# A graph network's second message layer in three sum passes, with the degree sums taken from TensorE

## The chip, the core and the metric

The kernel runs as one program on one core of a Trainium2 chip. The metric is the device time in microseconds (us) of one execution; lower is better. Engines are called by the profile's names: PE is TensorE (PEld its weight loads), DVE VectorE, ACT ScalarE, POOL GpSimd, SP the queue that issues most DMAs.

## What is computed

3125 nodes of 128 features, 100,000 edges (`src`, `dst`). First a block of two message layers, then a graph U-Net of nine convolutions ("in", three "dn", "bot", three "up", "out"). The change sits at the end of the first block and the beginning of the "in" convolution:

```
def _priv_conv(h, src, dst, n, Wl, bl, Wr, scale):
    xn = _l2norm(h)
    agg = jax.ops.segment_sum(xn[src], dst, num_segments=n)
    h_norm = jnp.linalg.norm(h, axis=-1, keepdims=True)
    out = _l2norm(agg) * h_norm * scale
    out = out @ Wl + bl + h @ Wr
    return _l2norm(out)
...
x = x + _L0_gnn_ref(h, ...)            # two such layers, 128 -> 256 -> 128 features
h = jnp.maximum(_layernorm(x, axis=-1), 0.0)
...
deg = 1.0 + jax.ops.segment_sum(ew, dst, num_segments=n)      # gcn_conv
dinv = jax.lax.rsqrt(deg)
norm = dinv[src] * dinv[dst] * ew
```

## The kernel before

The nodes are padded to 25 tiles of 128 (`TILES`). The program first builds the dense adjacency matrix in SBUF as 8-bit floats (`adj`: on the partitions the source within its tile, along the row tile after tile 3200 destinations, 3136 = `COLS` of them in use, self loops included; an entry is the count of edges times 0.125). Every `segment_sum` is then a product on PE: for each source tile t two f16 parts of the rows (high and low, `parts1[:, t, k]`) times `adj`'s row of t, in blocks of 448 destinations, 7 blocks (`BLOCKS`), each block a PSUM bank that gathers over the 25 tiles. PE keeps at most 7 such banks.

Layer 1 (`first_layer`) projects tile by tile: PE L2390, then DVE L1250, L1251 and the squares L1069, whose two tensor inputs are the same tile of SBUF. Layer 2 has 256 features in, m = 0 and 1. `fast_aggregate` (L2260) sums m = 0 in two passes of 4 and 3 blocks, then m = 1 likewise; DVE copies each finished block out of PSUM (L1049, `blocks_of`), and a pass waits until the banks that it writes were copied. PE is strictly in order, and so are the other engines: each is a queue written out by hand, with semaphores (`wait_ge`) between them.

After the last pass comes `second_layer`: PE projects the tiles two by two (L2344: sums times Wl, own rows times Wr), with the norms of the sums (L2271) after the fourth pair; DVE adds the bias (L1159) and combines (L1170, `combine`), ACT takes squares (L1971, `unit_squares`), DVE adds x (L1183, `add_x`), ACT squares again (L1978, `center_squares`), DVE makes the layer norm's factors (`scale_rows`), ACT writes the rows (L1986, `second_rows`), PE transposes them (L2363) and ACT keeps them (L1999). This goes in two parts of tiles, `LN_PARTS`. Between, PE sums the degrees (`degree_sums(0, False)`, L2305): 25 x 25 products of a 128x128 piece of `adj` with a column of ones. DVE turns them to 1/sqrt (L1031 to L1033).

Then `unet` begins with "in": PE products with the weight (L2762, groups of four tiles), ACT and DVE scale and split them to f16 (L2000, L1710), PE sums in three passes of 4, 2 and 1 blocks (L2800). DVE takes the blocks with `d_all`, the 1/sqrt degrees on every partition, which go out to DRAM (`dk_dram`) and come back broadcast. SP loads x again into `nodebuf` for `add_x`; in the kernel before this is done early, when `nodebuf` is free after the input's layer norm.

## Time and profile before

| | us |
|---|---|
| median of 3 runs | 1125.64 (1122.07 to 1128.34) |
| the profiled execution | 1124.67 |
| its span in the trace | 1122.5 |
| PE busy | 936.8 (83%) |
| DVE busy | 572.8 (51%) |
| ACT busy | 396.0 (35%) |
| POOL busy | 79.9 (7%) |

Times in the rows count from the start of the span. The profiled execution's own time is 2.2 us more than its span. The mean granted clock of PE is 0.918 of its full 2.4 GHz; the level under it is 1.2 GHz, 0.50 in the rows. A matmul's duration in a row is longer than its share of the engine, since matmuls are pipelined; a run of them is read by its length and count.

### The profile page before, as it was taken

Reading aid. Unit: us, or ns where it says so; the run is one execution under the profiler, and the core shown is the slowest. Engines: PE = TensorE matmul, PEld = TensorE weight load, DVE = VectorE, ACT = ScalarE, POOL = GpSimd, SP = SyncE. Lnnn points to the kernel's source line nnn. Section 1 sums busy time; section 2 is a strip of 40 time slices with the busy share of each in tenths; the row PEclk is TensorE's granted clock in tenths of the full one; section 3 lists DMA queues with packets and bytes.
Section 4 is the critical chain, followed back from the end, with each engine's and each line's share of the span. In section 5 each row is a group of like instructions: output and inputs, shape, how many; then the busy total and the mean of one; then the engine's idle time right before and its main releaser. Section 6 shows DMA issues by size and latency. Waiting matters only on the chain.

```text
span 1122.5 us, 17876 instructions
## 1 busy us (share of the span) xinstructions
PE 936.8 (83%) x7347; PEld 608.7 (54%) x7347; DVE 572.8 (51%) x1630; ACT 396.0 (35%) x869; POOL 79.9 (7%) x102
## 2 busy tenths in 40 slices
PE   0346999998799999979999978988876785778997
PEld 0335666766555556965465545655535443454654
DVE  4799999986921011642120267545542654445222
ACT  1538999982661000372010031544104402220300
POOL 2100000000000000000000000741014100020000
PEclk9759999999899999859999999998988787889999
DMA  6430000007100000011000002774114200140002
GB/s 192 136 84 1 1 2 1 2 1 318 49 1 1 1 1 1 2 68 52 1 1 1 1 1 61 258 214 141 27 25 119 60 1 1 30 175 29 33 1 59
DMA packets 39794, 60.39 MB, mean 54 GB/s; under 512 B 3822, under 2 KB 30721, under 8 KB 39192
## 3 DMA queue, kind: packets, MB, share of 16 engines
q1 hardware_dynamic: 31202, 38.17, 10.3%
q0 software_dynamic: 4592, 17.86, 5.2%
q10 hardware_dynamic: 3910, 3.12, 1.1%
q8 instruction: 61, 1.00, 0.4%
q14 instruction: 29, 0.24, 0.1%
HBM read 33.08 MB, written 30.85 MB: 57 GB/s over the span
## 4 chain that ended last, share of the span: by engine, by line
PE 55%; DVE 32%; ACT 5%; DMA 4%; issue 3%; POOL 1%; ACTq 0%; DVEq 0%; POOLq 0%; SPq 0%
PE psum L2800 24%; PE psum L2260 12%; DVE region L1010 7%; DVE region L1003 6%; PE psum L2568 4%; PE psum L2165 2%; DVE region L1517 2%; PE psum L2762 2%; DMA half_table<-region 2%; PE psum L2344 1%; PE psum L2190 1%; DMA nodebuf<-in_x 1%; POOL region L778 1%; DVE region L1251 1%; PE psum L2782 1%
## 5 line engine op out<-in xcount | busy, mean ns | idle before, releaser
L2800 PE MATMUL psum<-adj,region 128*128 128x448 fp8e4 x1050 | 201.8, 353 | 0.0
L2800 PEld LDWEIGHTS psum<-adj,region 128*128 128x128 f16 x1050 | 102.5, 98 | 92.9
L2260 PE MATMUL psum<-adj,region 128*128 128x448 fp8e4 x700 | 135.5, 355 | 3.1 <-DVE region L1244 3.1
L2190 PE MATMUL psum<-region 128*128 128x200 bf16 (+2 forms) x1176 | 111.0, 229 | 20.6 <-DVE region L1010 20.5
L2190 PEld LDWEIGHTS psum<-region 128*128 128x128 bf16 x1176 | 93.2, 99 | 55.0 <-DVE region L1010 30.4
L2260 PEld LDWEIGHTS psum<-adj,region 128*128 128x128 f16 x700 | 68.7, 98 | 66.8 <-issue 5.2
L2800 PE MATMUL psum<-region 128*128 128x448 fp8e4 (+2 forms) x426 | 83.7, 359 | 13.6 <-DVE region L1710 13.5
L1862 ACT ACTIVATE adj<-psum 128x400 fp8e4<-128x400 f32 x196 | 86.7, 518 | 19.4 <-PE psum L2194 18.8
L1010 DVE TENSOR_TENSOR region<-iota_key,region 128x1200 bf16<-128x1200 bf16 x147 | 92.7, 703 | 0.0
L2165 PE MATMUL psum<-adj,region 128*128 128x448 fp8e4 x350 | 91.7, 355 | 0.0
L778 POOL DMA_INDIRECT region<-adj_table,node_of x33 | 31.2, 945 | 848.3 <-DVE node_of L1647 731.3
L1003 DVE TENSOR_TENSOR region<-iota_lo,region 128x3072 bf16<-128x3072 bf16 x49 | 87.0, 1775 | 0.3 <-PE psum L2194 0.2
L2000 ACT ACTIVATE region<-psum 128x512 fp8e4<-128x512 f32 (+6 forms) x111 | 61.8, 599 | 71.5 <-PE psum L2782 24.9
L1736 DVE SCALAR_TENSOR_TENSOR region<-psum,unfit,region 128x448 f32<-128x448 f32 (+2 forms) x31 | 19.4, 661 | 123.4 <-PE psum L2800 107.5
L2568 PE MATMUL psum<-adj,nodebuf 128*128 128x448 fp8e4 x350 | 77.5, 376 | 0.4 <-issue 0.4
L1517 DVE CAST region<-psum 128x512 fp8e4<-128x512 f32 (+2 forms) x87 | 47.1, 599 | 58.8 <-PE psum L2645 29.4
L1845 ACT ACTIVATE region<-adj,below_full 128x3200 fp8e4<-128x3200 fp8e4 (+1 forms) x25 | 72.7, 2906 | 0.1
L2800 PEld LDWEIGHTS psum<-region 128*128 128x128 f16 x426 | 43.1, 102 | 51.4 <-issue 17.2
L2194 PE MATMUL psum<-ident 128*128 128x8 bf16 x392 | 67.5, 172 | 0.0
L2000 ACT ACTIVATE region<-psum,dcol 128x128 f16<-128x128 f32 x82 | 23.1, 377 | 121.2 <-PE psum L2762 104.3
L2078 ACT ACTIVATE region<-region,bn 128x512 f32<-128x512 f32 (+7 forms) x16 | 14.2, 948 | 126.1 <-DVE bn L1778 126.1
L1710 DVE SCALAR_TENSOR_TENSOR region<-psum,dcol,region 128x128 f16<-128x128 f32 x82 | 22.8, 345 | 67.5 <-ACT region L2000 67.5
(348 smaller groups left out, 1209.0 us busy)
## 6 DMA issues: line engine op xcount, KB each, us to landing
adj_table<-adj SPq DMA_DIRECT2D x1, 10000.0 KB, 27.2
edge_table<-edges SPq DMA_DIRECT2D x1, 4656.0 KB
region<-dk_dram SPq DMA_DIRECT2D x2, 1568.0 KB, 8.3
adj_table<-region SPq DMA_DIRECT2D x1, 2704.0 KB, 8.9
half_table<-region SPq DMA_DIRECT2D x2, 832.0 KB, 7.1
node_table<-region SPq DMA_DIRECT2D x1, 1650.0 KB, 8.4
xs_dram<-nodebuf SPq DMA_DIRECT2D x1, 1600.0 KB, 6.1
nodebuf<-xs_dram SPq DMA_DIRECT2D x1, 1600.0 KB, 6.1
```

Of the source, the lines that this page charges most:

```text
L1003: nc.vector.tensor_tensor(hot_lo[:, r].rearrange("p c j n i -> p (c j) n i"), iota_lo[:].rearrange("p (o n) i -> p o n i", o=1).broadcast_ ...
L1010: nc.vector.tensor_tensor(hot_key[:, r, c, :, k0:k1, :], iota_key[:, k0:k1, :].rearrange("p (o n) i -> p o n i", o=1).broadcast_to((P, BAT ...
L1517: v.tensor_copy(to, source, saturate=False).then_inc(dve_turned, 1)
L1845: nc.scalar.activation(excess_junk[:, :, 0:c1 - c0], adj_dests[:, :, c0:c1], ACT.Relu, bias=below_full[:], accum_out=excess[:, n:n + 1], s ...
L1862: nc.scalar.activation(adj_dests[:, :, 2 * WIN * q:2 * WIN * (q + 1)], psum[:, q % BUILD_BANKS, 0:2 * KEYS].rearrange("p (j t) -> p t j", ...
L2000: copy = lambda to, source, **k: nc.scalar.activation(to, source, ACT.Copy, **k)
L2165: last = pe.matmul(psum[:, 6 + b % 2, 0:BLOCK], parts0[:, t, k, :], adj[:, t * PAD + b * BLOCK:t * PAD + (b + 1) * BLOCK], start=(n == 0), ...
L2190: pe.matmul(psum[:, q % BUILD_BANKS, i * KEYS + k0:i * KEYS + k1], hot_lo[:, r, c, j, :, i], hot_key[:, r, c, j, k0:k1, i], start=(n == 0) ...
L2194: last = pe.matmul(loops, ident16[:], ident16[:, at:at + WIN], start=False, stop=True)
L2260: last = pe.matmul(psum[:, b, 0:BLOCK], weight(t, k), adj[:, t * PAD + b * BLOCK:t * PAD + (b + 1) * BLOCK], start=(t == 0 and k == 0), st ...
L2568: last = pe.matmul(psum[:, bank + b, 0:width], skip_parts[level][:, t, k, :], rows, start=(t == 0 and k == 0), stop=(t == LEVEL_TILES[leve ...
L2800: last = pe.matmul(psum[:, b, 0:width], here[:, t, k, :], rows, start=(t == 0 and k == 0), stop=(t == n_src - 1 and k == 1))
```

## The change

- The degrees are no longer sums on PE over 625 pieces. POOL adds the rows of `adj` of source tiles 0 to 9 onto each other, element by element (9 additions of 128x3136, 8-bit and f16 in, f16 out, into the first half of `nodebuf`); DVE does so for tiles 10 to 24 (14 additions, second half), after the first layer's last rows (`sum_lanes`). What is left, one row for each partition, PE sums over the partitions with 50 products with a column of ones (`sum_degrees`), before source tile 22 of m = 1's first pass. `nodebuf` is occupied until then, so SP loads x again after `deg_ready`.
- m = 1 is summed in three passes of 4, 2 and 1 blocks. The projections of a part's tiles, and its norms, stand between the products of the next pass (`PROJECT_AT`, `NORMS_AT`). There are three parts: tiles 0 to 13, 14 to 19, 20 to 24.
- ACT copies the blocks of the second and third pass out of PSUM itself (`take_blocks`), in its queue between the steps of the parts.
- The last part's later steps, and the transposes of tile groups 3 to 6, stand inside the first pass of "in".

```diff
-        EARLY = 4
-        LN_PARTS = ((0, 12), (12, TILES))
-        LN_LATE = 10
+        AGG_PASSES = ((0, 4), (4, 6), (6, BLOCKS))
+        LN_PARTS = ((0, 14), (14, 20), (20, TILES))
+        PROJECT_BANKS = (0, 1, 2, 3, 0, 1, 2, 3, 4, 5, 0, 1, 2)
+        PROJECT_FREED = (0, 0, 0, 0, 2, 4, 6, 8, 0, 0, 10, 12, 14)
+        PROJECT_AT = ({4: (0,), 6: (1,), 9: (2,), 11: (3,), 14: (4,), 16: (5,), 18: (6,)}, {9: (7,), 12: (8,), 15: (9,)})
+        NORMS_AT = (8, 18)
+        ROWS_FIRST = (2, 3, 1)
+        DEGREES_AT, TURN_DEGREES_AT = 22, 2
+        TURNED_FIRST = 3
+        TURN_BANKS_2 = (4, 5, 3, 7, 4, 5, 6)
+        TURNED_BEFORE = (1, 2, 3, 4, 5, 6, 7)
+        TURN_LAST_AT = {3: 0, 4: 4, 5: 8, 6: 12}
+        OWN_RING = 4
+        NORMS_BANK = (7, 7, 6)
+        NORMS_COL = 256
...
+        POOL_LANES = 10
...
             with sp.If(general < 1):
                 sp.dma_start(adj_table[0].rearrange("(t p) w -> p t w", p=P),
                              adj[:, :].bitcast(I32).rearrange("p (t w) -> p t w", t=TILES)).then_inc(adj_stored, DMA)
-                sp.wait_ge(centered, 3)
+                sp.wait_ge(deg_ready, 1)
+                load_x(sp, x_again)
+                sp.wait_ge(dkrows_ready, 1)
+                sp.dma_start(dk_dram[0], dk_rows_early).then_inc(dk_out, DMA)
+                sp.wait_ge(centered, 1 + len(LN_PARTS))
                 sp.dma_start(xs_dram[0], nodebuf[:]).then_inc(xs_out, DMA)
...
                 sp.wait_ge(dk_out, DMA)
                 row = dk_dram[0].rearrange("(v t) p -> v (t p)", v=2)
-                sp.wait_ge(proj_done, 2 * TILES)
-                sp.wait_ge(blocks_out, BLOCKS * FIRST_UNIT)
+                sp.wait_ge(squared, len(LN_PARTS))
                 sp.dma_start(d_all, row[0:1, 0:COLS].broadcast_to((P, COLS))).then_inc(db_in, DMA)
...
+                pool.wait_ge(bank_free, BUILD_BANKS + PAIRS)
+                for t in range(1, POOL_LANES):
+                    if t > 1:
+                        pool.wait_ge(lanes_step, t - 1)
+                    pool.tensor_tensor(lane_degrees[0][:, 0:COLS], adj[:, 0:COLS] if t == 1 else lane_degrees[0][:, 0:COLS],
+                                       adj[:, t * PAD:t * PAD + COLS], ALU.add).then_inc(lanes_step, 1)
+                pool.memset(lane_degrees[0][:, COLS:PAD], 0.0).then_inc(lanes_step, 1)
...
+            def sum_lanes():
+
+                lanes = lane_degrees[1][:, 0:COLS]
+                for t in range(POOL_LANES + 1, TILES):
+                    of = adj[:, POOL_LANES * PAD:POOL_LANES * PAD + COLS] if t == POOL_LANES + 1 else lanes
+                    step(nc.vector.tensor_tensor(lanes, of, adj[:, t * PAD:t * PAD + COLS], ALU.add))
+                nc.vector.memset(lane_degrees[1][:, COLS:PAD], 0.0).then_inc(lanes_summed, 1)
...
+            def early_degrees():
+
+                d, kept, deg = dcol[:, 0, 0, :], dcol[:, 0, 1, :], tiny[:, 10, :]
+                dve.wait_ge(deg_ready, 1)
+                step(nc.vector.tensor_scalar(deg, psum[:, 7, 0:TILES], 1.0 / COUNT, 1.0, ALU.mult, ALU.max))
+                rsqrt(d, deg, tiny[:, 11, :])
+                nc.vector.tensor_tensor(d, d, kept, ALU.mult).then_inc(dk_ready, 1)
...
-                blocks_of(1, 0, BLOCKS, first_agg(agg1t[:, 0, :]))
-                for b0, b1 in ((0, 4), (4, BLOCKS)):
-                    blocks_of(2, b0, b1, first_agg(agg1t[:, 1, :]))
-                    for b in range(b0, b1):
+                blocks_of(1, 0, 4, first_agg(agg1t[:, 0, :]))
+                blocks_of(1, 4, BLOCKS, first_agg(agg1t[:, 0, :]))
+                early_degrees()
...
+                def take_blocks():
+
+                    dve.wait_ge(agg_half, 4 + 1)
+                    for b in range(*AGG_PASSES[0]):
+                        first_agg(agg1t[:, 1, :])(b).then_inc(blocks_out, 1)
+
...
-                for g in range(EARLY):
-                    take_rows(g)
-                factor = agg_factor(1, norm1)
-                combine(0, LN_PARTS[0][1] // 2)
                 dve.wait_ge(x_again, 2 * DMA)
+                take_blocks()
+                add_squares(0)
+                dve.wait_ge(dk_turned, 1)
+                v.tensor_copy(dk_rows_early, psum[0:2 * TILES, 7, P:2 * P]).then_inc(dkrows_ready, 1)
+                combine_part(0)
                 add_x(0)
-                combine(LN_PARTS[1][0] // 2, LN_LATE)
+                add_squares(1)
                 scale_rows(0)
-                combine(LN_LATE, len(GROUPS2))
+                combine_part(1)
+                add_squares(2)
                 add_x(1)
+                combine_part(2)
                 scale_rows(1)
+                return add_x, scale_rows
...
+                        if i == 0 and t == 4:
+                            add_x(2)
+                        if i == 0 and t == 8:
+                            scale_rows(2)
...
+
+                    act.wait_ge(agg_half, 4 + n + 1)
+                    for b in range(*AGG_PASSES[n]):
+                        act.wait_ge(squares_added, b - 2)
+                        nc.scalar.activation(new_squares[:, b % 3, :], psum[:, b, 0:BLOCK], ACT.Square, scale=1.0 / (UNIT_SCALE * COUNT)).then_inc(sq_ready, 1)
+                        nc.scalar.activation(agg1t[:, 1, b * BLOCK:(b + 1) * BLOCK], psum[:, b, 0:BLOCK], ACT.Copy,
+                                             scale=1.0 / (UNIT_SCALE * COUNT)).then_inc(blocks_out, 1)
 
...
+                block_squares()
                 unit_squares(0)
+                take_blocks(1)
                 center_squares(0)
+                second_rows(0)
+                take_blocks(2)
                 unit_squares(1)
-                second_rows(0)
+                keep_turned(0)
                 center_squares(1)
+                keep_turned(1)
+                keep_turned(2)
                 second_rows(1)
-                for g, (t0, n) in enumerate(GROUPS4):
-                    act.wait_ge(h2_turned, g + 1)
-                    nc.scalar.activation(nodes_t[:, t0 * P:(t0 + n) * P], psum[:, g % 4, 0:n * P], ACT.Copy).then_inc(h2t_ready, 1)
                 copy = lambda to, source, **k: nc.scalar.activation(to, source, ACT.Copy, **k)
 
...
+                        if i == 0 and t == 4:
+                            unit_squares(2)
+                        if i == 0 and t == 8:
+                            keep_turned(3)
+                            center_squares(2)
+                        if i == 0 and t == 12:
+                            second_rows(2)
+                        if i == 0 and t % 4 == 0 and t >= 16:
+                            keep_turned(t // 4)
                         if i in POOLED:
...
-                    for d in range(TILES):
-                        for t in range(TILES):
-                            last = pe.matmul(psum[:, 7, d:d + 1], adj[:, t * PAD + d * P:t * PAD + (d + 1) * P], kept16[:, t:t + 1],
-                                             start=(t == 0), stop=(t == TILES - 1))
...
+                def sum_degrees():
+
+                    pe.wait_ge(lanes_summed, 1)
+                    pe.wait_ge(lanes_step, POOL_LANES)
+                    for t in range(TILES):
+                        for k in range(2):
+                            last = pe.matmul(psum[:, 7, t:t + 1], lane_degrees[k][:, t * P:(t + 1) * P], ones_col[:], start=(k == 0), stop=(k == 1))
+                    last.then_inc(deg_ready, 1)
+
+                for n, (b0, b1) in enumerate(AGG_PASSES):
+                    pe.wait_ge(blocks_out, BLOCKS + (4 if n == 0 else BLOCKS))
+                    for t in range(TILES):
+                        if n == 0 and t == DEGREES_AT:
+                            sum_degrees()
+                        if n == 1 and t == TURN_DEGREES_AT:
+                            turn_degrees(0)
+                        if n > 0 and t == NORMS_AT[n - 1]:
+                            part_norms(n - 1)
+                        for g in PROJECT_AT[n - 1].get(t, ()) if n > 0 else ():
+                            pe.wait_ge(blocks_out, 2 * BLOCKS + AGG_PASSES[n - 1][1])
+                            project_tiles(g)
+                        for k in range(2):
+                            for b in range(b0, b1):
+                                last = pe.matmul(psum[:, b, 0:BLOCK], parts1[:, t, k, P:2 * P], adj[:, t * PAD + b * BLOCK:t * PAD + (b + 1) * BLOCK],
+                                                 start=(t == 0 and k == 0), stop=(t == TILES - 1 and k == 1))
+                    last.then_inc(agg_half, 1)
+                pe.wait_ge(blocks_out, 3 * BLOCKS)
+                for g in range(LN_PARTS[2][0] // 2, len(GROUPS2)):
+                    if g == LN_PARTS[2][0] // 2 + 1:
+                        part_norms(2)
                     project_tiles(g)
...
+                pe.wait_ge(proj_done, TILES + LN_PARTS[1][1])
+                for g in range(TURNED_FIRST):
+                    turn_second(g)
...
+                        if i == 0:
+                            pe.wait_ge(h2t_ready, TURNED_BEFORE[g])
+                        if i == 0 and g in (2, 3):
+                            pe.wait_ge(proj_done, TILES + LN_PARTS[2][0] + 1 if g == 2 else 2 * TILES)
...
+                    if i == 0:
+                        pe.wait_ge(proj_done, 2 * TILES)
+                        pe.wait_ge(h2t_ready, TURNED_FIRST)
...
+                                for g in range(TURNED_FIRST, len(GROUPS4)) if i == 0 else ():
+                                    if t == TURN_LAST_AT[g]:
+                                        if g > 3:
+                                            pe.wait_ge(lo_ready, 4 * (g - 3))
+                                        turn_second(g)
```

PE, from the end of layer 2's m = 0 to "in". Before (L2260 the sums of both m, L2344 projections, L2271 norms, L2305 degrees, L2363 transposes, L2762 products of "in", L2800 its sums):

```order
L2260 MATMUL psum<-adj,region 128x448 x516
L2344 MATMUL psum<-region 128x128 x32
L2271 MATMUL psum<-ones,region 128x1 x25
L2344 MATMUL psum<-region 128x128 x68
L2305 MATMUL psum<-kept,adj 128x1 x625
L2363 MATMUL psum<-ident,region 128x128 x25
L2311 MATMUL psum<-ident,dcol 50x128
L2762 MATMUL psum<-weights,region 128x128 x12
```

PE after the change (L2370 sums of m = 0, L2484 of m = 1, L2467 degrees, L2447 projections, L2457 norms), the head of the stretch:

```order
L2370 MATMUL psum<-adj,region 128x448 x166
L2484 MATMUL psum<-adj,region 128x448 x176
L2467 MATMUL psum<-ones_col,nodebuf 128x1 x50
L2484 MATMUL psum<-adj,region 128x448 x32
L2414 MATMUL psum<-ident,dcol 50x128
L2484 MATMUL psum<-adj,region 128x448 x8
L2447 MATMUL psum<-region 128x128 x8
L2484 MATMUL psum<-adj,region 128x448 x8
L2447 MATMUL psum<-region 128x128 x8
L2484 MATMUL psum<-adj,region 128x448 x8
L2457 MATMUL psum<-ones,region 128x1 x14
L2484 MATMUL psum<-adj,region 128x448 x4
```

and its end (L2501 transposes, L2900 products of "in", L2946 its sums):

```order
L2484 MATMUL psum<-adj,region 128x448 x14
L2447 MATMUL psum<-region 128x128 x8
L2457 MATMUL psum<-ones,region 128x1 x5
L2447 MATMUL psum<-region 128x128 x12
L2501 MATMUL psum<-ident,region 128x128 x12
L2900 MATMUL psum<-weights,region 128x128 x12
L2501 MATMUL psum<-ident,region 128x128 x4
L2946 MATMUL psum<-adj,region 128x448 x8
L2900 MATMUL psum<-weights,region 128x128 x4
L2946 MATMUL psum<-adj,region 128x448 x24
L2501 MATMUL psum<-ident,region 128x128 x4
L2946 MATMUL psum<-adj,region 128x448 x8
```

The 625 rows of L2305 are gone, 50 of L2467 stand in m = 1's first pass, and what stood in one piece behind the sums stands between them.

DVE after the first layer's last rows. Before (L1049 takes blocks out of PSUM, L1153 adds squares):

```order
L1261 TENSOR_TENSOR tiny<-tiny 128x25
L1262 TENSOR_TENSOR tiny<-tiny 128x25
L1309 MEMSET region 128x64 x2
L1146 MEMSET region 128x64
L1049 TENSOR_SCALAR region<-psum 128x448 x11
L1153 TENSOR_TENSOR region<-region 128x448 x4
```

After (L1172 the additions, L1073 takes blocks, L1179 the first step on the degrees):

```order
L1346 MEMSET dcol 13x1
L1347 CAST last_real<-dcol 128x1
L1172 TENSOR_TENSOR nodebuf<-adj 128x3136
L1172 TENSOR_TENSOR nodebuf<-nodebuf,adj 128x3136 x13
L1173 MEMSET nodebuf 128x32
L1395 MEMSET region 128x64 x2
L1186 MEMSET region 128x64
L1073 TENSOR_SCALAR region<-psum 128x448 x7
L1179 TENSOR_SCALAR tiny<-psum 128x25
```

Fourteen additions now stand ahead of the first block copies.

ACT after the change, from the squares of the first part on (L2063 `unit_squares`, L2055 and L2056 `take_blocks`, L2070 `center_squares`, L2078 `second_rows`, L2087 `keep_turned`, L2101 the scaled rows of "in"):

```order
L2070 ACTIVATE region,tiny<-nodebuf,tiny 128x128 x14
L2078 ACTIVATE region<-nodebuf,tiny 128x128 x14
L2055 ACTIVATE region<-psum 128x448
L2056 ACTIVATE region<-psum 128x448
L2063 ACTIVATE region,tiny<-region 128x128 x6
L2087 ACTIVATE region<-psum 128x512
L2070 ACTIVATE region,tiny<-nodebuf,tiny 128x128 x6
L2087 ACTIVATE region<-psum 128x512 x2
L2078 ACTIVATE region<-nodebuf,tiny 128x128 x6
L2101 ACTIVATE region<-psum,dcol 128x128 x4
L2063 ACTIVATE region,tiny<-region 128x128 x5
L2101 ACTIVATE region<-psum,dcol 128x128 x4
```

The third pass's block (the second pair of L2055 and L2056) is taken behind the first part's 14 centred squares and 14 rows, and the first kept transposes, L2087, stand around the second part's squares.

## Rows read from the trace of the kernel before

**Rows 1.** Stretches: PE, PEld, DVE, ACT, POOL busy (instructions), granted clock, DMA.

```profile
343.00:374.00 31.00, 31.00 (x166) 16.03 (x164) 2.48 (x7) 2.55 (x5) 0.00 (x0) 1.00 0.00 1
440.50:471.70 31.20, 31.20 (x254) 31.19 (x253) 20.08 (x87) 7.46 (x37) 0.00 (x0) 0.89 0.01 1
471.70:488.30 16.60, 16.56 (x627) 16.48 (x626) 11.61 (x66) 13.61 (x65) 0.00 (x0) 0.65 0.11 40
488.30:502.50 14.20, 6.28 (x31) 5.01 (x27) 4.84 (x27) 11.26 (x36) 0.00 (x0) 0.50 0.18 75
```

**Rows 2.** PE in order of time: start, length, line, shapes, count, [idle before].

```profile
440.48 7.31 PE L2344 MATMUL psum<-region 128*128 128x128 f32 x64
447.62 6.07 PE L2271 MATMUL psum<-ones,region 128*128 128x1 f32 x50
453.55 18.26 PE L2344 MATMUL psum<-region 128*128 128x128 f32 x136
471.64 16.75 PE L2305 MATMUL psum<-kept,adj 128*128 128x1 bf16 x625
495.72 1.12 PE L2363 MATMUL psum<-ident,region 128*128 128x128 f32 x4 [4.67 <-ACT region L1986]
499.66 2.18 PE L2363 MATMUL psum<-ident,region 128*128 128x128 f32 x9 [2.82 <-ACT region L1999]
502.48 3.59 PE L2762 MATMUL psum<-weights,region 128*128 128x128 f32 x24 [0.43 <-ACT region L1999]
```

**Rows 3.** DVE in order of time, from the end of layer 1 to "in".

```profile
338.54 0.18 DVE L1262 TENSOR_TENSOR tiny<-tiny 128x25 f32<-128x25 f32 x1
346.16 2.22 DVE L1049 TENSOR_SCALAR region<-psum 128x448 f32<-128x448 f32 x4 [2.32 <-PE psum L2260]
374.47 1.69 DVE L1049 TENSOR_SCALAR region<-psum 128x448 f32<-128x448 f32 x3 [26.08 <-PE psum L2260]
502.57 0.08 DVE L1661 MEMSET dcol<- 128x25 f32 x1
503.51 0.16 DVE L1664 CAST last_real<-dcol 128x1 f16<-128x1 f32 x1
546.99 2.46 DVE L1736 SCALAR_TENSOR_TENSOR region<-psum,unfit,region 128x448 f32<-128x448 f32 x4 [17.48 <-PE psum L2800]
```

**Rows 4.** Two-input operations on DVE, by form: busy us, mean ns.

```profile
L1003 DVE TENSOR_TENSOR region<-iota_lo,region 128x3072 bf16<-128x3072 bf16 x49 | 87.0, 1775 | 0.3 <-PE psum L2194 0.2
L1069 DVE SCALAR_TENSOR_TENSOR region<-region 128x256 bf16<-128x256 f32 x25 | 10.3, 416 | 0.0
L987 DVE TENSOR_TENSOR region<-region 128x3200 f16<-128x3200 f32 x1 | 3.5, 3484 | 0.0
```

**Rows 5.** DVE, the flag that opens this branch of the program.

```profile
256.91 0.16 DVE L1112 TENSOR_TENSOR flag<-search 128x1 int32<-128x1 f32 x1
```

**Rows 6.** POOL in order of time.

```profile
3.75 2.28 POOL L745 IOTA iota_key<- 128x400 bf16 x1
7.62 0.29 POOL L765 CAST ident_h<-ident 128x128 f16<-128x128 f32 x1
```

**Rows 7.** PE by form: f16 columns of ones; and PE after a wait.

```profile
L2612 PE MATMUL psum<-ones_col,region 128*128 128x1 f16 x198 | 8.0, 165 | 1.4 <-DVE region L1517 1.1 <-issue 0.2
771.87 9.97 PE L2800 MATMUL psum<-region 128*128 128x391 fp8e4 x44 [3.80 <-DVE region L1710]
```

**Rows 8.** Stretches around that wait (columns as in rows 1).

```profile
774.00:776.00 2.00, 2.00 (x7) 0.91 (x6) 1.97 (x6) 0.77 (x3) 0.00 (x0) 0.50 0.79 284
776.00:780.00 4.00, 4.00 (x22) 2.21 (x21) 1.16 (x1) 0.00 (x0) 0.00 (x0) 0.88 0.00 0
```

**Rows 9.** SP's load of x, and a stretch at its end.

```profile
56.65 0.87 SPq L629 DMA_DIRECT2D nodebuf<-in_x  x1
66.00:67.00 1.00, 0.29 (x2) 0.00 (x0) 0.97 (x6) 0.67 (x2) 0.00 (x0) 0.50 0.40 98
```

**Rows 10.** ACT by form: the rows of a part.

```profile
L1986 ACT ACTIVATE region<-nodebuf,tiny 128x128 f32<-128x128 f32 x25 | 9.8, 479 | 2.7 <-DVE tiny L1195 2.7
```

More of the change, by code:

```diff
@@ L701, in _ @@
             with sp.Else():
+                load_x(sp, x_again)
                 loaded = 0
@@ new lines, in combine, with combine_part @@
+                def combine(g):
+                    t0, n = GROUPS2[g]
+                    dve.wait_ge(rows_taken, g + 1)
+                    for t in range(t0, t0 + n):
+                        v.scalar_tensor_tensor(tiles(out1)[:, t, :], project_slot(g, 0, n)[:, t - t0, :], tiny[:, 5, t:t + 1],
+                                               own_ring[:, g % OWN_RING, t - t0, :], ALU.mult, ALU.add).then_inc(proj_done, 1)
+                def combine_part(n):
+                    t0, t1 = LN_PARTS[n]
+                    g0, g1 = t0 // 2, -(-t1 // 2)
+                    for g in range(g0, g0 + ROWS_FIRST[n]):
+                        take_rows(g)
+                    agg_factors(n)
@@ L1164, in combine @@
                     for g in range(g0, g1):
[L1165 removed]
+                        if g0 + ROWS_FIRST[n] <= g + 1 < g1:
                             take_rows(g + 1)
[L1167 to L1171 removed]
+                        combine(g)
@@ L2433, in layers @@
                     first_layer()
[L2434 to L2436 removed]
+                    aggregate(1, lambda t, k: parts1[:, t, k, 0:P], lo1_ready, 1, between=turn_late)
                 if not by_edges:
```

156 lines of the change are left out of this document (79 added, 77 removed).

## The prediction

> **What bounds the kernel now.** I read the shares first: PE is busy for 83% of the span, and the chain that ended last is PE for more than half. So the question is what PE does between layer 2's m = 0 sums and the end of the first pass of "in", and what it waits for there. Everything that the change touches lies in this stretch or feeds it, except POOL's additions, which lie beside layer 1.
>
> In the stretches [rows 1] the reader is to see PE without a gap and at the full clock in the sums, and then two things: from 440.5 on the clock falls (0.89, 0.65, 0.50), and from 488.3 to 502.5 PE is busy for 6.3 us of 14.2. In order of time [rows 2] the work behind the sums is: projections 7.1 us up to the norms, norms 5.9, projections 18.1, degrees 16.7 us for 625 products, and the transposes. PE waits three times: 4.67 us for ACT's rows, 2.82 us for ACT to keep transposed tiles, 0.43 us more, together 7.9. DVE is done with layer 1 at 338.7 and then nearly idle: it takes four blocks at 346.2, and three at 374.5, when m = 0's second pass has ended. The first pass of "in" is over at 547.0 [rows 3]. From 374.3 to 547.0 are 172.7 us; I make the same stretch of the changed kernel.
>
> **What goes.** The 625 degree products, 16.7 us [rows 2]. The three waits, 7.9 us, go with their place; what waits instead is counted below. The projections of the first ten groups run between sums: in the row at the full clock 64 products take 7.1 us, 0.111 each, but the 136 after them took 18.1 us, 0.133 each, at a falling clock [rows 1, 2]. At the full clock these are 3.1 us shorter. Together 27.7 us.
>
> **What is added on PE.** 50 products with a column of ones. The f16 row has 198 in 8.0 us, 0.040 each [rows 7]: 2.0 us.
>
> **The additions on DVE.** This is the term that decides. An added operation has 3136 elements, one input of 8 bits, the other and the output f16. The trace has no such operation; the bounds are two rows [rows 4]. Where all three operands have 16 bits, 3072 elements took 1775 ns, 0.54 ns an element from start to start: 3136 elements would be 1.7 us. Where they have not (L987: f32 in, f16 out), 3200 elements took 3484 ns: 3136 would be 3.41, and in a run, where an operation overlaps the end of the one ahead a little, I take 3.34 us. I take 3.34, because an operand of another width than 16 bits is what sets the second row apart from the first; 1.7 stays as the lower end.
>
> The Trainium skill, VectorE: DVE Perf Modes, section "Mode 2×_1P", says that two results a cycle need 16-bit types throughout; the two rows agree with it, and no row shows an 8-bit input. By the page the sum takes the same 3.34.
>
> Fourteen of them are 46.8 us. They begin at 338.7, behind the eight small mask steps that moved here from "in" (502.57 to 503.67, 1.1 us) [rows 3], so DVE is free again at 386.6. Queued behind them are three memsets (0.3) and the copies of m = 0's first four blocks, 2.22 us [rows 3]; PE's first pass of m = 1 waits for the fourth, since it writes the same banks. It can begin at 389.3; before, it began at 374.3, without a wait. **PE stands still for 15.1 us.** That it has no other work then is in the order: nothing stands between L2370 and L2484.
>
> After a wait PE restarts at the lower level. At 771.87 it restarts after 3.8 us; the clock reads 0.50 to 776, and 0.88 on average to 780, so it is full from about 777 [rows 7, 8]: 5.1 us at half rate, 2.5 us lost. I add 2.5 us.
>
> **x loaded again.** SP now loads it when the degrees are in, before source tile 22 of m = 1's first pass, 4.4 us before that pass ends. The load in the trace was issued at 56.65 and its packets ended soon after 66 [rows 9], beside other loads of half its size; I take 8 us. DVE waits for it (`x_again`) ahead of its four block copies, and so gets at them 3.7 us after the pass has ended. PE reaches its first projection 3.4 us into the second pass, and needs these blocks: a wait of 2.5 us.
>
> **POOL.** Nine additions from about 259 (the flag is set at 257.1, [rows 5]). The bounds: a one-input cast of 128 elements took 0.29 us, 2.3 ns an element, the iota 2.28 us for 400, 5.7 ns [rows 6]. So 7 to 18 us each, 65 to 161 in all, over between 324 and 420. PE wants them at 389.3 plus 22 source tiles of 8 products (0.189 each), 422.5. Either end is hidden by the sums; I take it at nothing. Without DVE's late start PE would want them at 407.5, and the upper end would cost 12.
>
> **The parts' chains.** I followed the three queues with rows for each step: a row takes 0.39 us from start to start [rows 10], and I put a centred square at the same, a kept group at 0.5, a tile's combine at 0.26 and a factor chain at 3.6 (estimates, from the same functions before). PE's second pass (100 sums, 7 pairs of tiles, 14 norms, the turned degrees) takes some 35 us and its third 16. DVE keeps up with the pairs. Then: the third pass's block is taken by ACT behind the first part's squares and rows, PE waits 2.3 us; the product of "in" for group 1, 0.5; the transposes of group 3 need rows 12 to 15, and tiles 14 and 15 are part 1, whose factors DVE makes only after it has combined part 2: 3.1 us; the first scaled rows of "in" stand behind ACT's rows of part 1: 2.1; within the first pass the products of groups 3 and 4 wait for kept groups that stand behind part 2's steps in ACT's queue: 1.2 and 3.1. Together 12.3 us, in the place of 7.9. Bounds: nothing, if the queues run far enough apart, and 20, if each step is late by as much again.
>
> **The sum.** -27.7 + 2.0 + 15.1 + 2.5 + 2.5 + 12.3 = +6.7 us on the profiled execution's own 1124.67, which is 1.0 below the median: 1131.4. Behind the first pass of "in" nothing differs: `d_all` is sent when part 2 is squared, some 35 us before it is read.
>
> **Rivals.**
>
> *The additions take 1.7 us.* Then DVE is free at 363.6, ahead of 374.3, PE doesn't stand still, and its clock doesn't fall: 17.6 us less, 1113.8, faster. It decides from (374.3 - 2.5 - 339.8) / 14 = 2.3 us downwards. For it: two of three operands are 16-bit. Against: both rows [rows 4].
>
> *POOL shuts DVE out.* From 259 on DVE does layer 1, where it is the bound: some 14 small steps with two inputs in SBUF for the factors, then one for each of 25 tiles, L1069 [rows 4]. If such a step can't begin while a POOL addition reads SBUF, about one gets through per addition; after nine of at least 7 us DVE stands where it stood around 268, at 324. That is 50 us or so on the path to layer 2, 1180; at two steps per gap, 40 us. No row has POOL reading SBUF beside DVE at length. It makes the kernel slower from some 5 us of blocking on, and at the price above by far.
>
> The Trainium skill, SBUF — State Buffer, section "Who interferes with whom", has this rule: a VectorE instruction with two SBUF inputs and a GpSimd instruction that reads SBUF exclude each other for the whole of the first. No run shows it here. It is what speaks most against this change.
>
> *The chains hide.* If the 12.3 us of waits don't come, 1119; it is the sum with DVE's stall alone.
>
> **How the numbers follow.** No difference within 0.5% (1120.0 to 1131.3) can be told by a measurement of this kernel. Chances: my forecast 0.44 (its own range 1123 to 1142, and 0.3 of the 0.44 lies above 1131.3), short additions 0.26 (1107 to 1120), POOL's exclusion 0.21 (1150 to 1190), hidden chains 0.09 (1115 to 1122). Slower 0.3 + 0.21 = 0.51; faster 0.26 + 0.05 = 0.31; the rest 0.18. The range runs from 1108 to 1166, so that it leaves out most of the exclusion's upper part and little else.
>
> **What the profile will show.** Fourteen DVE additions from 339.8 in steps of 3.34 us; an idle PE in front of the first product of m = 1, released by DVE's fourth copy, and a clock of 0.5 behind it; layer 1 on DVE ending at 338.7 as before, if POOL doesn't hold it, or much later if it does, with L1069's successor stretched or started late; POOL's additions over before 420; the projections between sums at 0.11 us a product; six short waits of PE around the beginning of "in". I am wrong if the additions are short, or if layer 1 is stretched.

## The result and the profile after

The changed kernel takes 1174.5 us, the kernel before 1123.9 us (medians of four runs each): a ratio of 1.047, with an interval of 1.044 to 1.051. It is slower, by 50.7 us, and above the forecast range. The profiled execution has 1179.3 us and a span of 1177.4, 54.9 more than the span before.

POOL in order of time (start, length, engine, line, form, count, idle before) shows where the additions lie:

```profile
257.15 5.76 POOL L802 TENSOR_TENSOR nodebuf<-adj 128x3136 f16<-128x3136 fp8e4 x1 [211.84 <-DVE flag L1136]
262.99 47.04 POOL L802 TENSOR_TENSOR nodebuf<-nodebuf,adj 128x3136 f16<-128x3136 f16 x8
```

Nine additions, 5.88 us from start to start, under the 7 to 18 us that I had bounded; they end at 310. The kernel before has no POOL work here, and its DVE does the small steps of this stretch in 0.18 us each; one of them, and PE's wait for DVE there:

```profile
266.04 0.18 DVE L873 TENSOR_SCALAR tiny<-tiny 128x25 int32<-128x25 int32 x1
...
270.15 11.55 PE L2390 MATMUL psum<-region 128*128 128x256 f32 x40 [2.17 <-DVE region L1251]
```

DVE of the changed kernel in order of time beside the additions, and then up to m = 1 (same columns):

```profile
257.37 1.74 DVE L1143 TENSOR_TENSOR weights<-weights,psum 128x128 f32<-128x128 f32 x7 [1.20 <-PE psum L2432]
259.42 3.52 DVE L1355 CAST kept<-dcol 128x25 bf16<-128x25 f32 x1
...
269.31 5.47 DVE L906 TENSOR_SCALAR tiny<-tiny 128x25 f32<-128x25 f32 x1
274.81 0.18 DVE L896 TENSOR_SCALAR tiny<-tiny 128x25 int32<-128x25 int32 x1
275.02 5.62 DVE L897 TENSOR_SCALAR tiny<-tiny 128x25 int32<-128x25 int32 x1
280.68 0.18 DVE L899 TENSOR_TENSOR tiny<-tiny 128x25 f32<-128x25 f32 x1
280.90 5.63 DVE L900 SCALAR_TENSOR_TENSOR tiny<-tiny 128x25 f32<-128x25 f32 x1
...
381.58 0.18 DVE L1336 TENSOR_TENSOR tiny<-tiny 128x25 f32<-128x25 f32 x1
...
386.42 44.94 DVE L1172 TENSOR_TENSOR nodebuf<-nodebuf,adj 128x3136 f16<-128x3136 f16 x13
...
431.81 3.81 DVE L1073 TENSOR_SCALAR region<-psum 128x448 f32<-128x448 f32 x7
```

The steps over 25 columns from L906 on belong to the inverse square roots that DVE needs before its first combining step of layer 1 (L1325), and PE waits for that step to free its banks. Each has 25 elements a partition. Every second one has 0.18 us, and the one between is shown as 5.6 us, nearly the length of a POOL addition: it ends when the addition ends. So two steps get through for each addition here, until POOL has made its last. L1325 comes at 311.3, where it came at 269.6 before, and layer 1's last step, at 338.7 before [rows 3], is over at 381.8. The products of the weights at 257.37, with one input in PSUM, run freely: 1.74 us for seven, as before, nearly all of it beside POOL's first addition.

PE in order of time, the rows with waits over 1 us up to "in"'s first pass (two of 3.27 and 3.06 us inside layer 1, as long before, are left out), and the degrees:

```profile
311.81 11.55 PE L2527 MATMUL psum<-region 128*128 128x256 f32 x40 [42.51 <-DVE region L1325]
...
434.08 35.92 PE L2484 MATMUL psum<-adj,region 128*128 128x448 fp8e4 x176 [16.61 <-DVE region L1073]
469.83 1.39 PE L2467 MATMUL psum<-ones_col,nodebuf 128*128 128x1 f16 x50
...
482.96 3.36 PE L2447 MATMUL psum<-region 128*128 128x128 f32 x16 [4.04 <-DVE region L1073]
...
537.87 3.62 PE L2447 MATMUL psum<-region 128*128 128x128 f32 x16 [2.22 <-ACT region L2056]
...
549.25 2.05 PE L2900 MATMUL psum<-weights,region 128*128 128x128 f32 x16 [1.56 <-ACT region L2087]
553.11 0.63 PE L2501 MATMUL psum<-ident,region 128*128 128x128 f32 x4 [1.81 <-ACT region L2078]
555.95 3.17 PE L2946 MATMUL psum<-adj,region 128*128 128x448 fp8e4 x8 [2.22 <-DVE region L1790]
...
569.59 1.13 PE L2900 MATMUL psum<-weights,region 128*128 128x128 f32 x8 [1.65 <-DVE region L1790]
```

The first row is layer 1 standing still, 42.5 us where it was 2.2. The second is m = 1's first pass waiting for DVE's fourth copy, 16.6 us. The other six, 13.5 us together, are the wait for x (4.04) and five short waits of the parts.

The ledger of the spans: m = 1's first product starts at 434.1 instead of 374.3, 59.8 us later, of which 43.2 are layer 1 and 16.6 the wait. From there to DVE's first block of "in" are 168.7 us (602.75, before 546.99), 4.0 less than the 172.7 before, and what follows is 0.9 shorter: 59.8 - 4.0 - 0.9 = 54.9.

### The profile page after: what moved, and what is told of

It is laid out like the page before. It is cut to its first block, busy times and chain, and to the rows that moved or that the text cites. A ratio compares the mean times of both kernels' runs of the same rounds, so it can differ in the third digit from the quotient of the medians.

```text
span 1177.4 us, 16819 instructions
## 1 busy us (share of the span) xinstructions
PE 925.2 (79%) x6772; PEld 597.0 (51%) x6772; DVE 675.6 (57%) x1700; ACT 396.8 (34%) x872; POOL 132.4 (11%) x112
## 4 chain that ended last, share of the span: by engine, by line
PE 46%; DVE 40%; ACT 5%; DMA 4%; issue 3%; POOL 1%; DVEq 0%; ACTq 0%; SPq 0%; POOLq 0%
PE psum L2946 22%; DVE region L1034 6%; DVE region L1027 6%; DVE nodebuf L1172 4%; PE psum L2484 4%; PE psum L2703 3%; PE psum L2370 3%; DMA nodebuf<-in_x 2%; DVE tiny L900 2%; DMA half_table<-region 1%; DVE region L1600 1%; PE psum L2275 1%; PE psum L2447 1%; PE psum L2300 1%; PE psum L2900 1%
## 5 line engine op out<-in xcount | busy, mean ns | idle before, releaser
L2946 PE MATMUL psum<-adj,region 128*128 128x448 fp8e4 x1050 | 204.3, 355 | 2.2 <-DVE region L1790 2.2
L2946 PEld LDWEIGHTS psum<-adj,region 128*128 128x128 f16 x1050 | 103.0, 98 | 96.1 <-DVE region L1790 2.5
L2946 PE MATMUL psum<-region 128*128 128x448 fp8e4 (+2 forms) x426 | 81.9, 353 | 13.9 <-DVE region L1790 13.9
L2275 PE MATMUL psum<-adj,region 128*128 128x448 fp8e4 x350 | 90.4, 350 | 0.0
L2101 ACT ACTIVATE region<-psum 128x512 fp8e4<-128x512 f32 (+6 forms) x111 | 61.5, 599 | 75.5 <-PE psum L2840 25.3
L2484 PE MATMUL psum<-adj,region 128*128 128x448 fp8e4 x350 | 72.5, 366 | 16.6 <-DVE region L1073 16.6
L1600 DVE CAST region<-psum 128x512 fp8e4<-128x512 f32 (+2 forms) x87 | 47.2, 598 | 59.8 <-PE psum L2780 29.9
L2370 PE MATMUL psum<-adj,region 128*128 128x448 fp8e4 x350 | 70.7, 362 | 3.1 <-DVE region L1318 3.1
L2946 PEld LDWEIGHTS psum<-region 128*128 128x128 f16 x426 | 42.5, 101 | 50.8 <-issue 16.0
L2527 PE MATMUL psum<-region 128*128 128x256 f32 x100 | 29.0, 449 | 45.8 <-DVE region L1325 45.8
L2484 PEld LDWEIGHTS psum<-adj,region 128*128 128x128 f16 x350 | 35.3, 102 | 49.2 <-DVE region L1073 17.1
```

Of the source, the lines that this page charges most:

```text
L2101: copy = lambda to, source, **k: nc.scalar.activation(to, source, ACT.Copy, **k)
L2275: last = pe.matmul(psum[:, 6 + b % 2, 0:BLOCK], parts0[:, t, k, :], adj[:, t * PAD + b * BLOCK:t * PAD + (b + 1) * BLOCK], start=(n == 0), ...
L2370: last = pe.matmul(psum[:, b, 0:BLOCK], weight(t, k), adj[:, t * PAD + b * BLOCK:t * PAD + (b + 1) * BLOCK], start=(t == 0 and k == 0), st ...
L2484: last = pe.matmul(psum[:, b, 0:BLOCK], parts1[:, t, k, P:2 * P], adj[:, t * PAD + b * BLOCK:t * PAD + (b + 1) * BLOCK], start=(t == 0 and ...
L2946: last = pe.matmul(psum[:, b, 0:width], here[:, t, k, :], rows, start=(t == 0 and k == 0), stop=(t == n_src - 1 and k == 1))
```

## The experiments

Each run stands beside runs of the kernel before on the same chip. Runs 1, 2, 5 and 6 and runs 3, 4 and 11 were made on chips on which the kernel before took 1123.8 and 1124.4 us; their times are given as measured. Runs 7 to 10 were made on a chip on which every kernel took some 3.4% more (the kernel before 1162.6 us), nearly all of it behind "in"'s first pass; there only ratios and rows up to there are used, and us are the ratio times 1123.9. The time of runs 2, 3 and 4 is that of a single execution.

**1. Without POOL's additions.** PE takes over source tiles 0 to 9:

```diff
-                pool.tensor_tensor(lane_degrees[0][:, 0:COLS], ...)      # all nine
+                        for n, s in enumerate(range(POOL_LANES)):
+                            last = pe.matmul(psum[:, 7, t:t + 1], adj[:, s * PAD + t * P:s * PAD + (t + 1) * P], kept16[:, s:s + 1], ...)
```

> The changed kernel without POOL's nine additions: PE sums the rows of source tiles 0 to 9 straight from the adjacency matrix, 250 products of 128x1 and 25 for DVE's lanes, 275 where 50 stood (225 more at 0.0265 us, 6.0 us). DVE's fourteen additions stay in one piece. Theory 1, POOL's additions shut DVE out of layer 1: DVE ends layer 1 near 338.7 us again, 43 us earlier, PE still stands still for 15 to 17 us ahead of m = 1, and the time is 1174.5 - 43.9 + 6.0 = 1137 us. Theory 2, layer 1 is late for another reason (the store of the matrix to DRAM, the new order on PE or DVE): DVE ends layer 1 at 381 us as before and the time is 1180 us.

Measured: 1137.4 us, 1.012 (1.006 to 1.018). DVE's fourteen additions begin 42 us earlier, and PE's wait ahead of m = 1 is as long as it was; in order of time, DVE and PE:

```profile
340.86 3.43 DVE L1165 TENSOR_TENSOR nodebuf<-adj 128x3136 f16<-128x3136 fp8e4 x1
...
391.99 35.41 PE L2479 MATMUL psum<-adj,region 128*128 128x448 fp8e4 x176 [16.61 <-DVE region L1066]
```

The run is 37.1 us faster although PE has 225 products more, forecast at 6.0 us (in run 5, which has the same products, 275 take 7.1 us, where the 50 took 1.3). So POOL's additions cost some 43 us. It isn't the store of the matrix to DRAM or the new order, the other theory, since both are still there.

**2. Four POOL additions instead of nine.** The loop's end is 5 instead of `POOL_LANES`.

> POOL makes four additions instead of nine, PE sums source tiles 5 to 9 from the matrix (125 products more, 3.3 us). Theory 1, one whole POOL addition (5.9 us) for each pair of DVE steps: DVE is let go after four of them, at about 257 + 4 x 5.9 = 281 us, layer 1 ends near 355 us, and the time is 1174.5 - 5 x 5.9 + 3.3 = 1148 us. Theory 2, the two engines share the memory's speed and DVE's steps are merely slower: the delay is spread over all steps of layer 1 that lie beside POOL, none of them is as long as a POOL addition.

Measured: 1147.7 us. POOL ends at 279.9, and the last long step of DVE with it (274.33 + 5.62 = 279.95):

```profile
268.61 5.47 DVE L906 TENSOR_SCALAR tiny<-tiny 128x25 f32<-128x25 f32 x1
274.33 5.62 DVE L897 TENSOR_SCALAR tiny<-tiny 128x25 int32<-128x25 int32 x1
...
352.21 3.43 DVE L1172 TENSOR_TENSOR nodebuf<-adj 128x3136 f16<-128x3136 fp8e4 x1
```

From the flag to DVE's first addition are 96.9 us here, 126.9 with nine, 83.2 without POOL. So nine additions (52.9 us) cost 43.7 and four (23.4 us) cost 13.7: each further addition costs 6.0 us, its full length, and some 9.5 us of POOL's time are free, since DVE had 4.2 us to wait for PE there anyway and gets two steps through for each addition. It isn't a slowing in proportion, theory 2: the steps let through have 0.18 us as ever.

**3 and 4. POOL copies, and POOL fills, in the place of the additions.** Nine instructions of the same size each, nobody reads what they write:

```diff
-                    pool.tensor_tensor(lane_degrees[0][:, 0:COLS], ..., ALU.add)
+                    pool.tensor_copy(lane_degrees[0][:, 0:COLS], adj[:, t * PAD:t * PAD + COLS])        # run 3
+                    pool.memset(lane_degrees[0][:, 0:COLS], 0.0)                                        # run 4
```

> As the run without POOL's additions (1137 us, DVE ends layer 1 near 339 us), and in their place POOL makes nine copies of a row of the matrix into the free buffer, with one input in SBUF instead of two; nobody uses the result. Theory 1, whatever reads SBUF on POOL holds up DVE's steps that lie wholly in SBUF: DVE's small steps are stretched again, each to the end of a copy, and layer 1 ends later than 339 us by nearly nine copies' length. Theory 2, only POOL's two-input additions do: DVE ends layer 1 near 339 us.

> As the last one, but POOL fills the buffer nine times (writes only, no input). Theory 1, it is POOL's reads that hold up DVE's steps with two inputs in SBUF: of DVE's steps only those with one input in SBUF (the cast of the mask, the copies for the scores, the scaling by a number) may still be stretched, those with two (the square root's steps L892 to L894) last 0.18 us beside POOL, and layer 1 is late by less than half as many fills as there were additions. Theory 2, any work of POOL holds up any step of DVE that lies in SBUF: two-input steps are stretched as well.

Measured: copies 1154.5 us, fills 1148.0 us, where the run without POOL has 1137.4. POOL and DVE with the copies, in order of time:

```profile
256.68 25.86 POOL L802 CAST nodebuf<-adj 128x3136 f16<-128x3136 fp8e4 x9 [211.61 <-DVE flag L1134]
...
268.41 2.66 DVE L895 TENSOR_SCALAR tiny<-tiny 128x25 int32<-128x25 int32 x1
271.10 0.18 DVE L897 TENSOR_TENSOR tiny<-tiny 128x25 f32<-128x25 f32 x1
271.32 2.67 DVE L898 SCALAR_TENSOR_TENSOR tiny<-tiny 128x25 f32<-128x25 f32 x1
274.02 2.83 DVE L899 SCALAR_TENSOR_TENSOR tiny<-tiny 128x25 f32<-128x25 f32 x1
```

and with the fills:

```profile
256.98 24.89 POOL L802 MEMSET nodebuf<- 128x3136 f16 x9 [211.15 <-DVE flag L1134]
...
268.08 2.73 DVE L894 TENSOR_SCALAR tiny<-tiny 128x25 int32<-128x25 int32 x1
270.85 2.73 DVE L895 TENSOR_SCALAR tiny<-tiny 128x25 int32<-128x25 int32 x1
273.62 0.18 DVE L897 TENSOR_TENSOR tiny<-tiny 128x25 f32<-128x25 f32 x1
273.84 0.18 DVE L898 SCALAR_TENSOR_TENSOR tiny<-tiny 128x25 f32<-128x25 f32 x1
274.06 0.18 DVE L899 SCALAR_TENSOR_TENSOR tiny<-tiny 128x25 f32<-128x25 f32 x1
```

A copy holds DVE up as an addition does, for its own 2.87 us, steps with one input and with two; here one or two steps get through for each copy. Layer 1 is 16.6 us late by the same count as above (355.40 - 255.57 = 99.8, 83.2 without). Nearly nine copies' length, 25.9, was expected; I had left out the 9 us or so that are free as in run 2. A fill holds up the steps with one input in SBUF (L894 and L895, 2.73 us, the length of a fill) and lets those with two pass: nine in a row of 0.18 us go by, over within one fill. So with reads both kinds of DVE step are shut out, with writes alone only the one-input kind. The half of the expectation on the price, less than half as many fills as additions, holds: layer 1 is 10.9 us late (349.95 - 255.87 = 94.1), four fills.

This is the rule of the Trainium skill, SBUF — State Buffer, section "Who interferes with whom", which I had weighed: a DVE instruction with two SBUF inputs contends with a POOL instruction that reads SBUF, not with one that only writes. The section also says that DVE's copies, casts and operations with a scalar can take the shared pair. I had left that out; L894 and L895 beside the fills agree with it.

**5. DVE's additions parted.** As run 1, with six additions ahead of the first four copies and eight behind:

```diff
-                    sum_lanes()
+                    sum_lanes(POOL_LANES + 1, POOL_LANES + 1 + 6)
...
                 blocks_of(1, 0, 4, first_agg(agg1t[:, 0, :]))
+                sum_lanes(POOL_LANES + 1 + 6, TILES)
```

> As the run without POOL's additions, and DVE's fourteen additions are parted: six, the copies of m = 0's first four blocks, eight, the copies of the other three. Theory 1, the stall ahead of m = 1 is only the four copies' place behind the fourteen additions: the stall and the slow clock behind it go, 16.6 + 2.5 us less than the run without POOL, 1118 us. Theory 2, PE waits for something else there, or the eight additions behind the copies hold up the degrees: a stall stays in front of m = 1's first or second pass, or before its source tile 22, and the time stays over 1128 us.

Measured: 1118.5 us, 0.9955 (0.9924 to 0.9987), 18.9 less than run 1. No wait stands ahead of m = 1 any more:

```profile
373.33 33.46 PE L2481 MATMUL psum<-adj,region 128*128 128x448 fp8e4 x176
```

This run is also faster than the kernel before, by half a per cent, with an interval that ends just under 1.

**6. The lanes in the old order.** The kernel before, with run 5's additions and 275 products:

```diff
-                degree_sums(0, False)
+                    for s in range(10):
+                        pe.matmul(psum[:, 7, 64 + d:65 + d], adj[:, s * PAD + d * P:s * PAD + (d + 1) * P], kept16[:, s:s + 1], ...)
+                    last = pe.matmul(psum[:, 7, 64 + d:65 + d], lane_sums[:, d * P:(d + 1) * P], ones_col[:], ...)
```

> The kernel before, with only this changed: DVE adds the lanes of source tiles 10 to 24 (six additions, four block copies, eight additions), and PE sums the degrees with 275 products inside m = 1's first pass instead of 625 behind the projections; x is loaded again after that. Passes, parts and projections stand as before. Theory 1, the 625 products were work on the path: 16.7 us less and 7.3 more, 1123.9 - 9.4 = 1114.5 us. Theory 2, they only filled the time that the second part's chain of DVE and ACT steps takes behind the last projection (471.6 to 495.7 us): the first twelve transposes come 16.7 us earlier and the wait for ACT's rows behind them grows from 4.7 to about 21 us; with the 7.3 us inside the sums the time is 1131 us.

Measured: 1133.2 us, 1.008 (1.005 to 1.012), slower. PE in order of time, behind the last projection:

```profile
464.98 16.89 PE L2358 MATMUL psum<-region 128*128 128x128 f32 x136
491.40 1.09 PE L2376 MATMUL psum<-ident,region 128*128 128x128 f32 x4 [9.53 <-ACT region L2000]
...
505.87 1.12 PE L2376 MATMUL psum<-ident,region 128*128 128x128 f32 x4 [10.36 <-ACT region L2000]
509.81 2.19 PE L2376 MATMUL psum<-ident,region 128*128 128x128 f32 x9 [2.82 <-ACT region L2013]
```

From the end of the last projection to the transposes of the second part are 24 us here (481.9 to 505.9) and 24 before (471.8 to 495.7) [rows 2]. The 16.7 us of degrees lay inside them: taken away alone they are worth nothing, as theory 2 had it. What the run loses are the 275 products inside m = 1 (407.9 to 415.1, 7.2 us) and slower sums behind them: 174 in 35.6 us, where 176 take 33.5 at the full clock of run 5; the granted clock from 415 to 450 is 0.92.

**7. The new order alone.** The changed kernel without lanes, all 625 products before source tile 22 of m = 1's first pass.

> The changed kernel without any lane additions: PE sums the degrees with all 625 products, at the same place, before source tile 22 of m = 1's first pass. What is left of the change is the three passes, the three parts and the projections among the sums. Against the parted additions' run, 350 products more at 0.0265 us: 9.3 us. Theory 1, the order alone is worth 4 to 5 us less than nothing, since the short waits of the parts and the slow clock behind them cost what the old waits did, and the 16.7 us of the degrees no longer cover anything: 1118.5 + 9.3 = 1128 us, 4 above the kernel before. Theory 2, DVE's additions disturb the sums or the parts beside them (slower reads, late copies), so that taking them away gives part of the 9.3 back: 1120 us or less.

Measured: 1.0043 (1.0028 to 1.0059), 1128.7 us. Together with runs 5 and 6 these are the four corners: old order and all products 1, old order with lanes 1.008, new order with all products 1.004, new order with lanes 0.9955. Each half alone loses; the lanes are worth 0.9% once the order no longer needs the products as cover. That the lanes lose in the old order is shown only with the 275 products inside m = 1; left behind the projections, where the wait would cover them, they weren't tried.

**8. POOL's additions after layer 1.** DVE adds nothing, PE sums source tiles 10 to 24, POOL starts on DVE's last low rows:

```diff
                 pool.wait_ge(bank_free, BUILD_BANKS + PAIRS)
+                pool.wait_ge(lo1_ready, TILES)
```

> POOL makes its nine additions only after DVE's last low rows of layer 1 (near 338 us), DVE makes none, and PE sums source tiles 10 to 24 from the matrix (375 products and 25 for POOL's lanes, 125 more than with DVE's lanes: 3.3 us). Beside the additions DVE has only copies out of PSUM. Theory 1, POOL holds up only steps of DVE that read SBUF alone, and there are none: POOL ends near 392 us, ahead of source tile 22 at 407, PE has no stall at m = 1, and the time is 1118.5 + 3.3 = 1122 us. Theory 2, POOL's additions hold up every step of DVE: the first four copies come late by up to two additions each, and PE stands still for 5 us or more before m = 1, or at its second pass: 1127 us or more.

Measured: 0.998 (0.9965 to 0.9995), 1121.7 us. POOL lies beside DVE's copies out of PSUM and holds up none of them; they take 2.22 and 1.69 us as before [rows 3]:

```profile
339.01 5.78 POOL L803 TENSOR_TENSOR nodebuf<-adj 128x3136 f16<-128x3136 fp8e4 x1 [289.35 <-DVE region L1319]
344.87 46.67 POOL L803 TENSOR_TENSOR nodebuf<-nodebuf,adj 128x3136 f16<-128x3136 f16 x8
...
339.59 0.16 DVE L1348 CAST last_real<-dcol 128x1 f16<-128x1 f32 x1
...
346.61 2.22 DVE L1074 TENSOR_SCALAR region<-psum 128x448 f32<-128x448 f32 x4 [2.32 <-PE psum L2370]
374.91 1.69 DVE L1074 TENSOR_SCALAR region<-psum 128x448 f32<-128x448 f32 x3 [26.08 <-PE psum L2370]
```

The same nine additions that cost some 43 us in layer 1 cost nothing visible 80 us later: against run 7 this run is 7.0 us faster by the ratios, and has 225 products less. The cast at 339.59 is one-input and wholly in SBUF, lies inside POOL's first addition and isn't held up; it has a single column.

**9 to 11. How far it goes.** Eighteen additions on DVE (source tiles 6 to 24); on top of that, x waited for where it is added; on top of that, ACT takes the third pass's block in the middle of the first part's rows:

```diff
-        POOL_LANES = 10
+        POOL_LANES = 6
...
-                dve.wait_ge(x_again, 2 * DMA)
                 take_blocks()
...
                 combine_part(0)
+                dve.wait_ge(x_again, 2 * DMA)
                 add_x(0)
...
-                second_rows(0)
+                second_rows(0, (0, 8))
                 take_blocks(2)
+                second_rows(0, (8, LN_PARTS[0][1]))
```

> As the parted additions, but DVE adds the lanes of source tiles 6 to 24: six additions, four copies, twelve additions, and PE has 175 products instead of 275. By the row of 3.46 us an addition DVE is done at 339 + 18 x 3.46 + 2.2 = 403.5 us, ahead of source tile 22 at 407. Theory 1: 100 products less, 1118.5 - 2.7 = 1116 us. Theory 2, the three copies behind the twelve additions or the degrees come late: a stall before the second pass, 1118 us or more.

> As the run with eighteen additions, and DVE waits for x only before it adds it (after the first part's combine steps) and no longer before it takes m = 1's first four blocks. Theory 1, the wait of PE for these blocks (2.05 us at the first projection) was this wait's place, and goes together with the slow clock behind it: 2 to 3.5 us less than the run with eighteen additions, 1113 us. Theory 2, DVE or ACT is the next to be late in the second pass: PE waits as long at the norms or at the next pairs of tiles, and nothing is gained.

> As the run with eighteen additions and x waited for late, and ACT takes the third pass's block after 8 of the first part's 14 rows instead of behind all 14. Theory 1, PE's wait of 2.3 us behind the third pass is this place in ACT's queue alone: it goes with the slow clock behind it, 2.3 to 3.5 us less than that run, whose ratio to the kernel before was 0.991: 0.989 or less. Theory 2, the steps behind it (the second part's rows, that the fourth group of transposes waits for) set the end anyway: PE waits as much more there, and the ratio stays 0.991.

Measured: 0.9953 (0.9927 to 0.9978), 0.9914 (0.9880 to 0.9948) and 0.9925 (0.9898 to 0.9953). The four additions more bring 0.2 us against run 5 by the ratios, where 2.7 were expected; the intervals, 5 us wide, can't tell these apart. The wait for x in its new place goes, by the ratios with 4 us, which the intervals don't clearly separate either; in the trace the row of the first projection has no wait any more. Parting ACT's rows brings nothing: in order of time, PE behind the third pass in run 10 and then in run 11,

```profile
470.27 2.05 PE L2442 MATMUL psum<-region 128*128 128x128 f32 x16 [2.31 <-ACT region L2051]
...
480.02 2.05 PE L2897 MATMUL psum<-weights,region 128*128 128x128 f32 x16 [1.56 <-ACT region L2082]
```

```profile
470.30 2.05 PE L2443 MATMUL psum<-region 128*128 128x128 f32 x16 [1.07 <-ACT region L2051]
...
481.85 3.78 PE L2898 MATMUL psum<-weights,region 128*128 128x128 f32 x16 [3.33 <-ACT region L2082]
```

the wait of 2.31 us becomes 1.07, and the next one 3.33 instead of 1.56. Theory 2 stands: PE waits as much more there. The version of run 10 has the lowest ratio, 0.9% under the kernel before; runs 9 to 11 can't be told apart by their intervals.

## Why the prediction was wrong

The step that failed is the one on POOL. Under **POOL** the prediction said of its additions "Either end is hidden by the sums; I take it at nothing", and gave the exclusion of DVE 0.21 as a rival. The runs showed this rival to be what happens: nine additions from 257 to 310 us hold DVE up for 43 us at the head of layer 1, where DVE is what PE waits for. The forecast of 1131.4 and the 43.1 us that run 1 gives (37.1 and 6.0) make 1174.5, the time measured. That it fits so exactly is luck: the profiled execution took 1179.3, and its stretch behind m = 1's first product is 4.4 us longer than the sum has it (below).

The rival's own working gave 1180 with one step let through for each addition, and 40 us of delay at two; in the square root it is two. It too came near in part by luck. It took an addition at 7 us or more, and it has 5.88; and it had only DVE steps with two inputs held up, while of the nine stretched steps five have one input (L1355, L1288, L906, L897, L908). The 25 squares of layer 1 (L1069, now L1093), which it also named, weren't touched: POOL was done before the first of them. That no row had POOL reading SBUF beside DVE at length was no evidence against it: POOL's work in the trace before is set-up in the first 8 us and DMA issues, none of it beside layer 1, so that trace could bear on neither side. The rule of the Trainium skill that names just this case should then have weighed more than a fifth.

The other terms, by the names that the sum gives them:

- *The additions on DVE*, 3.34 us each taken: 3.46 from start to start (44.94 us for thirteen). The lower bound of 1.7 us is out. The wait before m = 1 was put at 15.1 us and is 16.6, and run 5 shows that the place in DVE's queue is all of it.
- *The clock behind that wait*, 2.5 us: 176 products take 35.92 us, and 33.46 us in run 11 without the wait, 2.46.
- *x*: a wait of 2.5 us forecast, 4.04 measured. DVE stood ready and waited for the load, as said; from the degrees to DVE's first copy are 9.5 us (471.2 to 480.7), where 8 were taken.
- *The parts' chains*: 2.3, 0.5, 3.1, 2.1, 1.2 and 3.1 forecast, at the places named 2.22, 1.56, 1.81, 2.22, none and 1.65: 9.5 of 12.3.
- *The projections at the full clock* was too good. Behind the waits and the norms the clock falls again; in the stretches (PE, PEld, DVE, ACT, POOL busy, granted clock, DMA share, GB/s)

```profile
485.00:505.00 20.00, 20.00 (x120) 15.98 (x119) 6.43 (x28) 2.00 (x12) 0.00 (x0) 0.78 0.01 3
505.00:530.00 25.00, 25.00 (x172) 18.36 (x171) 11.81 (x61) 10.10 (x49) 0.00 (x0) 1.00 0.00 1
530.00:560.00 30.00, 22.19 (x142) 17.89 (x141) 21.85 (x116) 18.33 (x68) 0.00 (x0) 0.86 0.01 2
```

it reads 0.78 and 0.86 with a stretch of 1.00 between, which is 20 x 0.22 + 30 x 0.14 = 8.6 us of full clock lost, part of it in idle time. Sixteen products of L2447 take 3.36 and 3.62 us behind a wait and 1.95 in the middle. From m = 1's first product to the end of "in"'s first pass the sum gives 172.7 - 27.7 + 2.0 + 2.5 + 2.5 + 12.3 = 164.3 us; measured 168.7.
- *What goes*, the 16.7 us of degrees: right in the new order only. Run 6 shows that in the old one they were cover, and the sum was right because it booked the waits of the new order beside them.

## What to carry over

Before work is given to an idle POOL, look at what DVE does in the same microseconds, instruction by instruction: in these runs POOL was free beside DVE's reads of PSUM and cost nearly its full length beside small steps wholly in SBUF on the path. An in-order queue wants the long optional work parted around the short copy that another engine waits for. And work that ends just before a wait is cover: price its removal by the chain beside it, not by its length; it may pay only together with a change of that chain's place.

## What the runs showed of the hardware

- While a POOL instruction reads SBUF, DVE's steps that lie wholly in SBUF stand still to its end, even steps of 25 columns (5.6 us beside an addition, 2.7 to 2.8 beside a copy, instead of 0.18). A cast of a single column was not held (0.16 us, run 8). Between two POOL instructions that wait for one another, one or two such steps get through. A fill by POOL stops DVE's one-input steps (2.73 us) and not its two-input ones (0.18 us).
- DVE's instructions with an input in PSUM aren't touched by it: seven products of 0.25 us beside POOL's first addition (1.74 us in all, as before), and the block copies of run 8.
- The profile shows a step that is shut out as busy, not as waiting: DVE's busy time between 250 and 300 us rose from 39.6 to 46.6 while it did a third of the instructions (56 instead of 167). A mean of one instruction in such a group, or the share of busy time, hides it; the row in order of time shows it.
- POOL's addition of 128x3136 takes 5.88 us, DVE's 3.46, with an 8-bit and an f16 input and an f16 output.
